# First layer of a delta-rule and attention stack: the gate product as one rounded product over 96 rows, and the second half of the output projection in two parts

## The chip, the cores and the metric

One core of one Trainium2 chip runs the whole program. The time is the device time of one execution, in microseconds (us); lower is better. Engines are named as in the profile: PE (TensorE matmuls), PEld (its weight loads), DVE (VectorE), ACT (ScalarE), POOL (GpSimd), SP (SyncE, which issues transfers here).

## The reference

The program computes four layers on x of 16 batches x 512 tokens x 512 features; the change touches only the first one. Of that one:

```python
q = silu(x @ Wq.T); k = silu(x @ Wk.T); v = x @ Wv.T      # 16 heads of 32
beta = 2.0 * sigmoid(x @ Wbeta.T)
k = k * rsqrt(sum(k * k, -1) + EPS)
o = delta_rule(q, k, v, beta)                # a state per head, carried over the 512 tokens
gate = sigmoid(x @ Wg1.T @ Wg2.T)            # Wg1 is 32 x 512, Wg2 is 512 x 32
og = o * gate; og = og * rsqrt(mean(og * og, -1) + EPS) * g_norm
x = x + og @ Wo.T                            # x was layer-normalised on the way in
```

The gate is a product of two thin matrices: g1 = x @ Wg1.T has 32 features, and the gate product takes them to 512.

## The kernel before, in words

`delta_rule_layer` (from line 47) works on spans of 256 tokens, two to a batch, 32 in all. Everything is held with features on the partitions. `over_spans` unrolls one step per span, and each step works on up to five spans at once: it finishes `now` (solve, chain over chunks of 64 tokens), writes out `behind`, inverts triangles for `ahead`, projects `further`, and loads `beyond`. 29 of the 32 steps have both `behind` and `further`, 30 have `further`. Two spans are projected in `begin` before the first step. Nothing loops at run time: every instruction of every step stands in the instruction stream, and the order on each engine is the order of the Python calls. The engines meet through semaphores alone.

Accurate products are made of rounded ones: a number is split into its rounded part (`_hi`, type fp32r) and the rest (`_lo`), and `split3` (lines 38 to 42) adds hi x hi, hi x lo and lo x hi. All large projections go that way (features, `project_k`, `project_q`, `project_gb`, `project_v`, `output`). A few small ones are plain fp32 products instead, `project_gate` (L542) among them; the profile records each plain fp32 product as two matmuls and two weight loads. The products of the solve, of `query_corrections` (L646), `transitions` (L658), `without_state` (L682), `state_inputs` (L692) and `chain` (L703 and L709) are also plain fp32, and tiny: 32 to 64 rows, 32 to 64 columns, 64 products a call (16 and 16 in a chain call).

PE's order in a step from the end of the solve on: `project_gb(further)`, `query_corrections(now)` (L646), `output(behind, 0)` (12 products of 512 columns), `transitions(now)` (L658), `project_q(further, 1)` (24 of 256), `without_state(now)` (L682), `output(behind, 1)` (12 of 512), `state_inputs(now)` (L692), `chain(now, 0)`, `key_sums(further, 0)` (L529), `chain 1`, `project_gate(further, 0)`, `chain 2`, `project_gate(further, 1)`, `chain 3`, `key_sums(further, 1)`, `output_sums(now)` (L719), then `project_v`, `key_rows` (L557), `triangles` (L569) and `project_v`. A chain call adds gt x state for the next state (L703), then the state's part of the output (L709); call c + 1 waits for `state_ready`, which DVE gives in `advance` (L933), before the gated output (L939).

PSUM banks are shared by hand. BB holds g1 and beta of `project_gb`, then `output(behind, 1)`, then half of the gate; so `output(behind, 1)` waits until ACT has taken beta, and `project_gate(further, 1)` until DVE has added the residual (`add_residual`, L953).

ACT's `take_gb` copies g1 (L313) and makes beta (L316) out of BB. DVE fills its free time with the columns of the inverse of `ahead` (`invert`, L886 and L889), cut into named stretches that stand between the steps that PE waits for. SP loads and stores and carries triangles and inverses through DRAM.

## Time and profile before

| | |
|---|---|
| median of 3 runs | 4955.77 us (4949.72 to 4962.0) |
| profiled execution, its own time | 4960.62 us |
| its span, first to last instruction | 4958.5 us |
| PE busy | 4588.3 us, 93% |
| DVE busy | 3635.6 us, 73% |
| ACT busy | 2411.9 us, 49% |
| first layer | about 0 to 2010 us of the span |
| granted clock, mean | 0.969 |

Busy time counts from the start of an instruction to its end. PE's are pipelined and overlap, so the distance from the start of one to the start of the next says what it costs in a row of them. "issue" as the end of idle time means that the engine waited for nothing that the profile shows.

### The profile page before, as it was taken

The page shows a single profiled execution, that of the slowest core. Times are in us where ns is not written, and L with a number is a line of the kernel's source. Part 1 is how long each engine was busy: PE and PEld are TensorE (multiplying, and loading weights), DVE is VectorE, ACT ScalarE, POOL GpSimd, SP SyncE. Part 2 cuts the span into 40 slices and gives each one's busy share as a digit, 9 for nine tenths or more (in the row PEclk, how much of TensorE's full clock was granted, in tenths as well). Part 3 has the DMA queues.
Part 4 walks back from the last instruction along what each step waited for, and adds up shares of the span by engine and source line. Part 5 has one row for each costly group of instructions (what it writes and reads, how often), then busy time and mean ns, then how long its engine had stood idle before and what let it go on. Part 6 is the DMA issues. An engine that isn't in the chain of part 4 may idle for free.

```text
span 4958.5 us, 144788 instructions
## 1 busy us (share of the span) xinstructions
PE 4588.3 (93%) x63104; PEld 3209.3 (65%) x63104; DVE 3635.6 (73%) x7890; ACT 2411.9 (49%) x4592; POOL 720.6 (15%) x909
## 2 busy tenths in 40 slices
PE   7999999999999998699999999999999999999998
PEld 7787777777787776555655654664664665565564
DVE  6677777766676665578778778778778877877876
ACT  3333343333343332366466456457456546546645
POOL 0000000000000000121221221221221122122121
PEclk8999999999999998899999999999999999999999
DMA  2222222222222221100000000000000000000000
GB/s 85 55 63 72 64 69 65 67 67 66 65 63 63 63 63 49 62 2 18 18 1 19 18 2 18 18 2 18 18 18 2 18 18 2 18 18 2 18 10 10
DMA packets 352134, 171.76 MB, mean 35 GB/s; under 512 B 300016, under 2 KB 300784, under 8 KB 350736
## 3 DMA queue, kind: packets, MB, share of 16 engines
q1 hardware_dynamic: 342528, 145.20, 10.9%
q10 hardware_dynamic: 8976, 17.30, 1.2%
q8 instruction: 499, 8.18, 0.7%
q14 instruction: 131, 1.07, 0.1%
HBM read 93.74 MB, written 67.63 MB: 33 GB/s over the span
## 4 chain that ended last, share of the span: by engine, by line
PE 43%; DVE 11%; ACT 2%; issue 1%; POOL 1%; DMA 1%; SPq 0%; DVEq 0%; ACTq 0%; POOLq 0%
PE row_psum L1738 9%; PE row_psum L1713 9%; PE row_psum L40 5%; DVE smax L2000 5%; PE row_psum L42 5%; PE row_psum L41 5%; PE row_psum L1726 4%; PE row_psum L1786 1%; DVE xr_lo L1861 1%; PE row_psum L1766 1%; DVE probs L1980 1%; PE row_psum L1500 1%; DVE stats L1827 1%; POOL rstd L1297 1%; DMA q_stack<-shift 1%
## 5 line engine op out<-in xcount | busy, mean ns | idle before, releaser
L2000 DVE TENSOR_REDUCE smax<-row_psum 128x1 f32<-128x512 f32 x2048 | 1270.5, 685 | 91.7 <-PE row_psum L1713 88.6
L1434 ACT ACTIVATE probs<-row_psum 128x512 f32<-128x512 f32 x2048 | 1091.8, 603 | 352.2 <-PE row_psum L1726 332.9
L1713 PE MATMUL row_psum<-k_stack,q_stack 64*128 64x512 f32 (+1 forms) x2048 | 738.1, 437 | 50.8 <-DVE smax L2000 24.5
L1726 PE MATMUL row_psum<-q_stack,k_stack 64*128 64x512 f32 (+1 forms) x2048 | 733.3, 458 | 22.6 <-ACT probs L1434 8.1
L1713 PEld LDWEIGHTS row_psum<-k_stack,q_stack 64*128 64x128 f32 (+1 forms) x2048 | 350.8, 186 | 503.8 <-DVE smax L2000 372.9
L1738 PE MATMUL row_psum<-probs,v_aug 128*32 128x512 f32 x4096 | 538.9, 603 | 1.6 <-ACT av_sb L1450 0.4
L1726 PEld LDWEIGHTS row_psum<-q_stack,k_stack 64*128 64x128 f32 (+1 forms) x2048 | 319.3, 184 | 225.8 <-ACT probs L1434 155.7
L889 DVE TENSOR_TENSOR lane_t<-lane_t,lane_p 128x30 f32<-128x30 f32 (+14 forms) x960 | 318.5, 332 | 32.9
L40 PE MATMUL row_psum<-wf_hi,xr_hi 128*128 128x320 f32 (+1 forms) x1024 | 331.9, 324 | 4.7 <-DVE xr_lo L1861 3.2
L886 DVE TENSOR_TENSOR lane_p<-lane_t 128x30 f32<-128x30 f32 (+14 forms) x960 | 316.4, 330 | 23.5
L42 PE MATMUL row_psum<-wf_hi,xr_lo 128*128 128x320 f32 (+1 forms) x1024 | 319.0, 312 | 0.0
L41 PE MATMUL row_psum<-wf_lo,xr_hi 128*128 128x320 f32 (+1 forms) x1024 | 317.9, 310 | 0.0
L265 POOL TENSOR_TENSOR o_lo<-og_both,o_hi 128x512 fp32r<-128x512 f32 x64 | 93.2, 1476 | 1331.3 <-DVE tri L904 1239.1
L1311 POOL TENSOR_TENSOR xs<-xs,av_n 128x256 f32<-128x256 f32 x128 | 94.0, 735 | 1236.1 <-DVE av_n L1994 1236.1
L369 ACT ACTIVATE og_both<-og_both 128x512 f32<-128x512 f32 x64 | 40.4, 632 | 470.6 <-DVE og_both L939 470.6
L1401 ACT ACTIVATE q_stack<-row_psum 128x512 fp32r<-128x512 f32 x256 | 153.8, 607 | 152.7 <-PE row_psum L1663 151.2
L40 PE MATMUL span_bank<-x_hi,w_hi 128*128 128x256 f32 x768 | 223.9, 292 | 0.0
L41 PE MATMUL span_bank<-x_lo,w_hi 128*128 128x256 f32 x768 | 214.4, 279 | 1.1 <-issue 1.1
L42 PE MATMUL span_bank<-x_hi,w_lo 128*128 128x256 f32 x768 | 214.4, 279 | 1.1 <-issue 1.1
L1990 DVE RECIPROCAL av_rc<-row_psum 128x16 f32<-128x16 f32 x128 | 32.2, 251 | 245.6 <-PE row_psum L1786 245.6
L40 PEld LDWEIGHTS row_psum<-wf_hi,xr_hi 128*128 128x128 f32 x1024 | 192.9, 188 | 29.1 <-issue 20.6
L41 PEld LDWEIGHTS row_psum<-wf_lo,xr_hi 128*128 128x128 f32 x1024 | 193.7, 189 | 0.6
(215 smaller groups left out, 9999.8 us busy)
## 6 DMA issues: line engine op xcount, KB each, us to landing
x_sp<-in_x ACTq DMA_DIRECT2D x33, 512.0 KB, 4.2
tri_dram<-tri SPq DMA_DIRECT2D x256, 64.0 KB, 2.0
lane_t<-tri_dram SPq DMA_DIRECT2D x32, 512.0 KB, 4.6
inv_dram<-lane_t SPq DMA_DIRECT2D x32, 512.0 KB, 2.7
inv_b<-inv_dram SPq DMA_DIRECT2D x256, 64.0 KB, 2.3
x_res<-in_x SPq DMA_DIRECT2D x32, 512.0 KB, 3.8
x<-x_res SPq DMA_DIRECT2D x32, 512.0 KB, 3.9
xs<-x SPq DMA_DIRECT2D x16, 1024.0 KB, 5.5
```

Source lines behind the costliest of these rows:

```text
L40: pe.matmul(out, a_hi, b_hi, start=first, stop=False)
L41: pe.matmul(out, a_hi, b_lo, start=False, stop=False)
L42: return pe.matmul(out, a_lo, b_hi, start=False, stop=last)
L886: mark(dve.tensor_tensor(prod, lane_t[:, 0:m, m:m + 1].to_broadcast([P, m, n]), lane_t[:, m:m + 1, m + 1:NB].to_broadcast([P, m, n]), ALU. ...
L889: mark(dve.tensor_tensor(lane_t[:, 0:m, m + 1:NB], lane_t[:, 0:m, m + 1:NB], prod, ALU.add))
L1311: pool.tensor_tensor(xq, xq, av_n[:, :, :, :].rearrange("p t h e -> p t (h e)"), ALU.add).then_inc(adot_added, 1)
L1401: act.activation(q_stack[:, m, :], ps[:, (HP + m) % STACK_BANKS, :], ACT.Copy).then_inc(qstack_ready, 1)
L1434: act.activation(probs[:, h % PROBS, tt, :], ps[:, m % STACK_BANKS, :], ACT.Exp, scale=float(DH) ** -0.5).then_inc(exp_ready, 1)
L1713: pe.matmul(ps[:, bank, :], q_stack[rows, qt, P * st:P * st + P], k_stack[rows, kv, :], start=True, stop=True).then_inc(max_mm, 1)
L1726: pe.matmul(ps[:, m % STACK_BANKS, :], k_stack[rows, kv, P * tt:P * tt + P], q_stack[rows, qt, :], start=True, stop=True).then_inc(score_m ...
L1738: last = pe.matmul(ps[32 * e:32 * e + 32, 6, :], v_aug[:, tt, h % NKV, :], probs[:, h % PROBS, tt, :], start=tt == 0, stop=tt == NT - 1)
L2000: dve.tensor_reduce(smax[:, g, st:st + 1], ps[:, bank_of("max", NT * g + st), :], AX.X, ALU.max).then_inc(max_ready, 1)
```

## The change

Three edits, all in the first layer. The gate product takes one rounded product with 96 rows in place of a plain fp32 product with 32: rows 0 to 31 hold g1 rounded, 32 to 63 the rest of g1, 64 to 95 g1 rounded once more, against weights rounded, rounded and rest. ACT makes the third part by a copy, DVE the second by a subtraction; the weights are loaded three times and split once at the start. The second half of the output projection runs two of its four input blocks before `state_inputs` and two after. DVE adds the residual of that half after `advance(now, 0)`.

```diff
-        g2 = sb("g2", [HD, D])
+        g2 = sb("g2", [3 * HD, D], F32R)
-        g1_beta = sb("g1_beta", [HD + H, SPAN])
-        g1, beta_t = g1_beta[0:HD, :], g1_beta[HD:HD + H, :]
+        g1 = sb("g1", [3 * HD, SPAN], F32R)
+        beta_t = sb("beta_t", [H, SPAN])
...
-            sp.dma_start(g2[:, :], w_g2).then_inc(c_in, 16)
+            for part in range(3):
+                sp.dma_start(g2_raw[HD * part:HD * part + HD, :], w_g2).then_inc(c_in, 16)
...
+            def split_g2():
+                act.wait_ge(c_in, 128)
+                act.activation(g2[:, :], g2_raw, ACT.Copy).then_inc(w_hi_ready, 1)
...
             def take_gb(b, s, first=False):
                 act.wait_ge(gb_proj, at(b, s, 1, 1))
-                act.activation(g1, BB[0:HD, 0:SPAN], ACT.Copy).then_inc(g1_ready, 1)
+                act.activation(g1[0:HD, :], BB[0:HD, 0:SPAN], ACT.Copy).then_inc(g1_ready, 1)
                 if not first:
                     act.wait_ge(beta_out, at(b, s, 16, 0))
-                act.activation(beta_t, BB[HD:HD + H, 0:SPAN], ACT.Tanh, scale=0.5).then_inc(beta_ready, 1)
+                act.activation(beta_t[:, :], BB[HD:HD + H, 0:SPAN], ACT.Tanh, scale=0.5).then_inc(beta_ready, 1)
+                act.wait_ge(g1_ready, at(b, s, 2, 1))
+                act.activation(g1[2 * HD:3 * HD, :], g1[0:HD, :].bitcast(F32), ACT.Copy).then_inc(g1_ready, 1)
...
             def project_gate(b, s, n, behind=None):
                 if n == 0:
                     pe.wait_ge(q_ready, at(b, s, 2, 1))
-                    pe.wait_ge(g1_ready, at(b, s, 1, 1))
+                    pe.wait_ge(g1_ready, at(b, s, 2, 2))
+                    pe.wait_ge(g1_lo_ready, at(b, s, 1, 1))
...
                     last = pe.matmul((BA, BB)[n][:, SPAN * g:SPAN * g + SPAN], g2[:, P * f:P * f + P],
-                                     g1, start=True, stop=True)
+                                     g1[:, :], start=True, stop=True)
...
-            def output(b, s, t, further, ahead):
+            def output(b, s, t, further, ahead, inputs=range(KT)):
-                if further:
+                if further and inputs[0] == 0:
                     if t == 0:
                         pe.wait_ge(ksilu_ready, at(*further, 2, 2))
                     else:
                         pe.wait_ge(beta_ready, at(*further, 1, 1))
+                        pe.wait_ge(g1_lo_ready, at(*further, 1, 1))
...
-                pe.wait_ge(ohi_ready, at(b, s, TS, t + 1))
-                pe.wait_ge(olo_ready, at(b, s, TS, t + 1))
-                for k in range(KT):
+                if inputs[0] == 0:
+                    pe.wait_ge(ohi_ready, at(b, s, TS, t + 1))
+                    pe.wait_ge(olo_ready, at(b, s, TS, t + 1))
+                for k in inputs:
...
-                last.then_inc(wo_mm, 1)
+                if inputs[-1] == KT - 1:
+                    last.then_inc(wo_mm, 1)
...
             begin (PE), each span:
-                    pe.wait_ge(c_in, 96)
+                    pe.wait_ge(c_in, 128)
+                    pe.wait_ge(w_lo_ready, 4)
...
                 without_state(*now)
                 if behind:
-                    output(*behind, 1, further, ahead)
+                    output(*behind, 1, further, ahead, range(KT // 2))
                 state_inputs(*now)
+                if behind:
+                    output(*behind, 1, further, ahead, range(KT // 2, KT))
                 chain(*now, 0)
...
+            def split_g2(place):
+                rows = slice(2 * HD, 3 * HD)
+                dve.wait_ge(w_hi_ready, place)
+                dve.tensor_tensor(g2[rows, :], g2_raw[rows, :], g2[rows, :].bitcast(F32), ALU.subtract).then_inc(w_lo_ready, 1)
...
+            def split_g1(b, s):
+                dve.wait_ge(g1_ready, at(b, s, 2, 1))
+                dve.tensor_tensor(g1[HD:2 * HD, :], BB[0:HD, 0:SPAN], g1[0:HD, :].bitcast(F32), ALU.subtract).then_inc(g1_lo_ready, 1)
...
                 correct_queries(*now)
+                if further:
+                    split_g1(*further)
                 invert_ahead("queries")
                 if behind:
                     add_residual(*behind, 0)
                 invert_ahead("transitions")
+                invert_ahead("inputs")
+                advance(*now, 0)
                 if behind:
                     add_residual(*behind, 1)
-                invert_ahead("inputs")
-                advance(*now, 0)
                 invert_ahead("chain0")
```

## Rows read from the trace of the kernel before

**Rows 1.** The page: span, busy times, and the queue that carries PE's instructions.

```profile
span 4958.5 us, 144788 instructions
PE 4588.3 (93%) x63104; PEld 3209.3 (65%) x63104; DVE 3635.6 (73%) x7890; ACT 2411.9 (49%) x4592; POOL 720.6 (15%) x909
...
q8 instruction: 499, 8.18, 0.7%
```

**Rows 2.** Windows, middle of the first layer: busy (x count) of PE, PEld, DVE, ACT, POOL.

```profile
190.00:1900.00 1710.00, 1629.09 (x41658) 1347.19 (x41656) 1199.49 (x2951) 655.73 (x1138) 107.53 (x112) 0.96 0.26 65
```

**Rows 3.** ACT's copy of g1, one a step: least, median, most ns, first and last start.

```profile
L313 ACT ACTIVATE g_beta<-span_bank x28: 376/376/377, 239.3 to 1863.0; 32x256 f32<-32x256 f32 x28
```

**Rows 4.** Groups of PE, 200 to 1900 us, with the idle time before them.

```profile
L709 PE MATMUL span_bank<-q_eff,state 32*32 32x64 f32 x3616 | 88.7, 235 | 20.8 <-issue 20.7
L703 PE MATMUL span_bank<-state,gt 32*32 32x32 f32 x3616 | 58.9, 202 | 16.7 <-issue 16.7
```

**Rows 5.** Timeline of PE, dense stretch of one step: start, length, line, count [idle].

```profile
1010.63 1.48 PE L646 MATMUL span_bank<-tri,uw 64*32 64x64 f32 x128
...
1024.91 0.45 PE L703 MATMUL span_bank<-state,gt 32*32 32x32 f32 x32
1025.18 0.30 PE L709 MATMUL span_bank<-q_eff,state 32*32 32x64 f32 x4
1027.06 0.64 PE L709 MATMUL span_bank<-q_eff,state 32*32 32x64 f32 x28 [1.58 <-issue]
1027.62 1.13 PE L529 MATMUL span_bank<-sq,head_ones 128*128 128x512 f32 x2
1028.68 0.45 PE L703 MATMUL span_bank<-state,gt 32*32 32x32 f32 x32
```

**Rows 6.** DMA over 1023.5 to 1032.7 us, 40 slices; then the queue over 190 to 1900.

```profile
GB/s 0 0 0 0 71 0 0 0 249 383 392 410 410 374 45 18 0 0 0 0 71 0 71 178 125 107 276 321 401 374 276 98 27 27 0 0 0 0 71 0
...
q8 instruction: 327, 5.36, 1.3%
```

**Rows 7.** Windows from the end of one such stall to the end of another.

```profile
970.85:1027.05 56.20, 53.47 (x1400) 45.13 (x1401) 41.07 (x100) 23.02 (x40) 3.85 (x4) 1.00 0.28 69
1027.05:1065.11 38.06, 34.27 (x761) 27.54 (x761) 22.00 (x50) 18.73 (x31) 2.94 (x2) 1.00 0.37 86
```

**Rows 8.** Timeline of PE at the second gate call of the same step.

```profile
1031.62 1.12 PE L542 MATMUL span_bank<-g_beta,g 32*128 32x256 f32 x4
1032.68 0.23 PE L703 MATMUL span_bank<-state,gt 32*32 32x32 f32 x3
```

**Rows 9.** Timeline of PE, end of a rounded projection of 256 columns.

```profile
1001.95 0.28 PE L41 MATMUL span_bank<-x_lo,w_hi 128*128 128x256 f32 x1
1002.07 0.28 PE L42 MATMUL span_bank<-x_hi,w_lo 128*128 128x256 f32 x1
1002.27 0.24 PE L587 MATMUL span_bank<-uw,tri 32*32 32x64 f32 x1
```

**Rows 10.** Timeline of DVE, same step.

```profile
1012.15 1.42 DVE L923 TENSOR_TENSOR q_eff<-kq,span_bank 128x256 f32<-128x256 f32 x4 [0.54 <-PE span_bank L646]
1023.79 0.69 DVE L953 TENSOR_TENSOR x_res<-x_res,span_bank 128x512 f32<-128x512 f32 x1 [0.40 <-PE span_bank L42]
1026.48 0.28 DVE L933 TENSOR_TENSOR state<-state,span_bank 128x128 f32<-128x128 f32 x1
1029.65 0.42 DVE L939 SCALAR_TENSOR_TENSOR og_both<-gate,span_bank 128x256 f32<-128x256 f32 x1
1036.25 0.20 DVE L895 COPY lane_t<-lane_b 128x32 f32<-128x32 f32 x1
```

**Rows 11.** Timeline of ACT, same step, after beta.

```profile
1013.60 0.60 ACT L320 ACTIVATE kq<-span_bank 128x512 f32<-128x512 f32 x1 [2.08 <-DVE q_eff L923]
```

**Rows 12.** Timeline at the start: PE's first gate, DVE's last weight split.

```profile
30.55 1.99 PE L542 MATMUL span_bank<-g_beta,g 32*128 32x256 f32 x8
...
26.05 2.29 DVE L822 TENSOR_TENSOR w_lo<-tri,w_hi 128x2048 fp32r<-128x2048 f32 x1 [0.66 <-ACT w_hi L288]
```

More of the change, by code:

```diff
@@ L106, in delta_rule_layer @@
         lane_t = sb("lane_t", [P, NB, NB])
+        g2_raw = lane_t[0:3 * HD, :, :].rearrange("p j i -> p (j i)")[:, D:2 * D]
         stage_gb = lane_t[:, :, :].rearrange("p j i -> p (j i)")[:, 0:KT * (HD + H)]
@@ L128, in delta_rule_layer @@
         xlo_ready = sem("xlo_ready"); kproj = sem("kproj"); ksilu_ready = sem("ksilu_ready")
-        gb_proj = sem("gb_proj"); g1_ready = sem("g1_ready")
+        gb_proj = sem("gb_proj"); g1_ready = sem("g1_ready"); g1_lo_ready = sem("g1_lo_ready")
         beta_ready = sem("beta_ready"); beta_out = sem("beta_out"); res_loaded = sem("res_loaded")
@@ L193, in to_lanes @@
                 sp.dma_start(beta_dram.rearrange("u h i -> h u i"),
-                             beta_t.rearrange("h (u i) -> h u i", i=NB)).then_inc(beta_out, 16)
+                             beta_t[:, :].rearrange("h (u i) -> h u i", i=NB)).then_inc(beta_out, 16)
                 for t in range(TS):
@@ L402, in begin @@
                     if span is first:
-                        split_weight(WV, c_in, 96)
+                        split_g2()
+                        split_weight(WV, c_in, 128)
                     take_k(*span, 1)
                     if span is first:
-                        split_weight(WO, c_in, 96)
+                        split_weight(WO, c_in, 128)
                     take_gb(*span, first=span is first)
@@ L755, in begin @@
                     key_sums(*span, 1)
-                    pe.wait_ge(w_lo_ready, NW + 1)
+                    pe.wait_ge(w_lo_ready, NW + 2)
                     project_v(*span, 0)
@@ L961, in begin @@
                 split_gb(3)
-                split_weight(WV, 4)
-                split_weight(WO, 5)
-                dve.wait_ge(c_in, 96)
+                split_g2(4)
+                split_weight(WV, 5)
+                split_weight(WO, 6)
+                dve.wait_ge(c_in, 128)
                 mark(dve.tensor_scalar(gnorm_half[:, :], gnorm_half[:, :], 0.5, None, ALU.mult))
+                split_g1(*first)
                 statistics(*second)
@@ L970, in begin @@
                 split_x(*second)
+                split_g1(*second)
                 statistics(*third)
```

## The prediction

> **What bounds the kernel now.** I read the page first: PE is busy 93% of the span [rows 1]. The windows view then shows the first layer by itself: between 190 and 1900 us PE is busy 1629.1 of 1710 us [rows 2], DVE 1199.5 and ACT 655.7. PE bounds this layer, and every step waits for PE's order. A step takes (1863.0 - 239.3) / 27 = 60.14 us [rows 3], and 29 steps are affected by all of the change.
>
> The second thing to see is what PE's idle time is. The groups view puts 20.8 and 16.7 us of it before L709 and L703, nearly all ended by "issue" [rows 4]. The timeline shows one case: in the middle of a row of equal products, after 4 of 32 records of L709, PE stands still for 1.58 us, and no semaphore is waited for there in the code [rows 5]. I take this for a lack of instructions. Three facts carry it. The queue named "instruction" moves 8.18 MB in 499 packets, 16 KB each [rows 1], and PE has 126,208 recorded instructions, so one packet is close to 253, say 256 with the unrecorded waits. Between the ends of such stalls the records of PE and PEld are 2801 and 1522 [rows 7]; with some 15 semaphore instructions each (the code's waits put about 16 into a step) these are 11 and 6 times 256. And the DMA slices of 0.23 us show single packets (71 GB/s in a slice) near 1024.5, 1028.2 and 1032.3 us [rows 6]: the stall of 1027.06 ends some 2.5 us after a packet started, and the next packet starts 1.1 us after the stall's end. So a block of 256 instructions is asked for when PE's queue enters the block before it, and can be used about 3.7 us later (3.6 to 4.1 between packets). A block that PE runs through in less ends in a stall.
>
> Where can that be? A step has 1468 matmul records, as many loads and 16 waits: 2952 instructions, 11.5 blocks [327 packets for 28.4 steps, rows 6]. From `query_corrections` at 1010.63 [rows 5] to the end of the chain, 0.93 us behind 1032.68 [rows 8], stand 826 records, or 6.5 blocks, in 23.0 us: with the stall of 1.58 taken off, 21.4 us of work, 3.3 us a block. That is below 3.7. The two groups of rows 4 alone have (20.8 + 16.7) / 28.4 = 1.3 us of idle a step; from start to start, which also counts what a record's drawn-out end covers, and over all groups, I put the stalls at 2.3 us a step and the step without them at 58.0.
>
> **The gate product.** Before: from its first record to the next chain's is 1.06 us for 4 records [rows 8], twice a step, 2.11 us in all. After: 2 records each. A rounded product of 256 columns costs 0.12 us in a row, and 0.20 where tiny products follow [rows 9]. With 0.12 + 0.20 for each pair and some 0.03 for the first's start: 0.35 us twice a step, hence 2.11 - 0.70 = 1.4 at the least. But the old 1.06 holds a start and a hand-over too, and without them the new pair is 0.24; so at most 2.11 - 0.24 = 1.87. I take 1.75, nearer to the upper end, for records of the old product lie 0.22 apart inside it, and the rest of its time is start and hand-over that stay hidden in neither. 30 steps and two spans of `begin`. In `begin` the 8 records take 1.99 us [rows 12]; I take 1.4 us off each.
>
> **Its price.** ACT gets one copy of 32 x 256: 0.38 us [rows 3] and a wait for its own earlier copy. ACT then idles 2.08 us until q_eff [rows 11], so it costs nothing; without that cover it would be 0.38 x 30 = 11 us. DVE gets a subtraction of 32 x 256 out of PSUM: at least 0.28 (L933, 128 columns), at most 0.42 (L939, 256 columns) [rows 10]; I take 0.4, the same column count. It is placed right behind q_eff (1012.15 to 1013.57) and delays the inverse and the residual behind it in DVE's queue. DVE has 0.40 us idle before the residual of the second half [rows 10], which the move frees as well, so it fits; without cover 12 us. PE's new wait before `output(behind, 1)` asks for this subtraction, done by about 1014 (q_eff ends at 1013.6), while that product starts some 3 us before its end at 1023.8 [rows 10]; so nothing stands queued behind a real wait. At the start, two more transfers on SP and two small splits come before DVE's last split ends at 28.3 us; g1's rest is then ready near 29.3, the gate starts at 30.55 [rows 12]. Nothing.
>
> **The move.** Six products (1.5 us) go from before `state_inputs` to behind it. PE's work is the same. For DVE the state of chunk 0 is taken at 1026.48, though PE had its part of it done by 1025.4: the residual (0.69) and its wait (0.40) stood before it [rows 5, 10]. With the residual behind `advance`, DVE is ready. That gives PE nothing where `key_sums` (1.06 us) lies between chain 0 and chain 1 anyway; it pays for the subtraction. On SP the store of `behind` goes 3 us later, behind it the load of 512 KB (the two busy stretches of slices in rows 6) and `from_lanes`, which waits for the inverse until 1036.4 [rows 10] in any case; nobody waits longer. The other effect is on blocks: `state_inputs` and chain 0 are the densest run (192 records in 2.4 us), and 1.5 us of slow products between them lets one block arrive. Lower bound 0, upper bound the stalls in that run, about 1 us a step; since the block count and the work of the whole stretch stay, I take 0.2.
>
> **What the blocks give back.** The stretch loses 1.75 us and four records: 19.6 us for 6.45 blocks, 3.0 us each. Were it bound by blocks alone it would take 6.45 x 3.7 = 23.9 us, no less than now, and the gain would be nought; were there no such bound, all of 1.75 would arrive. Between the ends I walked a step, block by block: the time from 40 instructions ahead of a block's edge to the next edge, against 3.7 us (4.2 in the solve, where transfers are dense; 40 is my choice, since with it the walk meets the measured step). For before this gives 60.4 us a step against 60.1 measured. After, a step has 2952 - 8 + 1 = 2945 instructions (one more for the fourth wait of `output`), which is 11 blocks and 129: the edges fall in two sets of places in turn, half a block apart, and hardly drift. One set has an edge at the end of `without_state` and one before the second gate: 885 to 1012 in records has 2.9 us of work (0.8 us stall), 1140 to 1267 has 2.6 (1.1 us). The other set falls better. The walk gives about 60.5 and 58.5 us in turn, 59.5 on average, so 0.9 us less a step, 2.3 us of stalls having become 3.2.
>
> The Trainium skill (Runtime: NRT & Kernel Launch, "Instruction fetch mechanics") gives the same 16 KiB blocks, but says that the fetch is hidden because the sequencer issues more slowly than blocks arrive. The rows speak against it here. By that rule the gate's whole saving would arrive: rival 1.
>
> **Sum**, against the profiled execution: 29 x 0.93 = 27, the first step (gate alone) 1, `begin` 2.8, DVE now binding by about 0.1 us between chains 2 and 3 (its 0.28 + 0.42 [rows 10] and 0.6 of inverse are 1.3 us a link against PE's 1.2) gives back 3. Together -28: 4960.6 becomes 4932.6. That execution lay 4.85 us above the median, so 4928 as a median. The last steps and the other layers stay.
>
> **Rivals.**
> 1. The saving arrives whole: 30 x 1.75 + 2.8 = 55, to 4901. For it: the stalls fall in other engines' shadow; the move spreads blocks. Against it: the counts in multiples of 256 [rows 7]. With all present chain stalls gone too it would be 4875; I give that little.
> 2. The blocks take all: the stretch stays as long as it is, only `begin` gains, and DVE's 3 us come on top: 4955.8 - 2.8 + 3, or up to 5 us less: about 4953. For it: packets come every 3.6 to 4.1 us without a pause in the dense stretch.
> 3. Slower: DVE becomes the bound between q_eff and chain 0. It has under 1.5 us idle there [rows 10], and the subtraction with its wait costs 0.4 to 0.9. If the blocks take all and DVE is late by 0.8 us before chain 1, 30 x 0.8 = 24 - 3: 4977. It decides from the point where the state of chunk 0 is given later than `key_sums` ends. Against it: the residual leaves the same place.
> 4. It does not do what it says: a product over 96 rows at the old cost. 4955. The rounded products of 128 rows in the same stream speak against it.
>
> **Chances.** Forecast (4913 to 4941) 0.55; rival 1 0.23; rival 2 0.14 with rival 4; rival 3 0.05; the rest lies between. A measurement of this kernel tells about 0.3%, 15 us, from no change. Faster by more: 0.81, same 0.14, slower 0.05. The range reaches from near rival 1 to near rival 2: 4897 to 4948.
>
> **What would show it.** L542 with 128 records, chain to chain 0.3 us over a gate. Stalls ended by "issue" grow in the chain to 3 us a step, ends of stalls still multiples of 256 apart, long and short steps in turn. DVE waits for L703 less. Wrong if steps are all 58.4 us (rival 1), or if "issue" takes 4 us a step (rival 2), or if PE waits for DVE's state by 0.5 us or more (rival 3).

## The result, and the profile after the change

The median of four runs is 4903.71 us (4896.4 to 4908.7), beside 4952.75 us for four runs of the kernel before. The ratio is 0.9897 with a 95% interval of 0.9876 to 0.9917. That is 51 us faster by the ratio, where 28 were forecast: the direction was right and the time lies in the range, but the size was forecast at about half.

The profiled execution took 4907.11 us. The page of the kernel after answers to [rows 1]:

```profile
span 4905.3 us, 144631 instructions
PE 4526.2 (92%) x62976; PEld 3166.9 (65%) x62976; DVE 3651.2 (74%) x7923; ACT 2423.4 (49%) x4625; POOL 720.1 (15%) x909
q8 instruction: 499, 8.18, 0.7%
```

PE has 128 products and 128 loads fewer (four a step and in each span of `begin`), DVE and ACT 33 instructions more. The instruction queue still moves 499 packets. The first layer is where all of it happened: the next layer's first product starts at 1969.5 us, before it was 2022.8. From there to the end both kernels take the same time (2935.8 and 2935.7 us).

Next the windows of the middle of that layer, as [rows 2], ACT's copy of g1 once a step, as [rows 3], and PE's groups from 200 to 1900 us, as [rows 4]:

```profile
190.00:1900.00 1710.00, 1608.94 (x42735) 1336.39 (x42734) 1248.64 (x3069) 679.59 (x1187) 111.37 (x115) 0.98 0.26 67
...
L319 ACT ACTIVATE g<-span_bank x28: 375/375/375, 236.7 to 1817.0; 32x256 fp32r<-32x256 f32 x28
...
L719 PE MATMUL span_bank<-q_eff,state 32*32 32x64 f32 x3744 | 80.3, 217 | 5.5 <-issue 5.5
L713 PE MATMUL span_bank<-state,gt 32*32 32x32 f32 x3713 | 60.7, 195 | 31.0 <-issue 29.4 <-DVE state L958 1.7
L702 PE MATMUL span_bank<-uw,rhs 64*32 64x32 f32 x3712 | 41.8, 200 | 14.3 <-issue 13.8
L552 PE MATMUL span_bank<-g 96*128 96x256 f32 x112 | 28.1, 332 | 0.0
```

A step takes (1817.0 - 236.7) / 27 = 58.53 us, 1.6 less than before. Three things are to be seen. L552 has no idle time of its own: the gate product is cheap. The idle time ended by "issue" has not gone: it moved from L709 (now L719, 20.8 to 5.5) to the chain's other product (16.7 to 31.0) and to L702, `state_inputs` (1.5 to 14.3). And two numbers changed that the prediction gave no term: one L719 product takes 217 ns where it took 235 in [rows 4], and the granted clock, the column behind POOL, rose to 0.98 from 0.96 [rows 2].

PE in one step of the kernel after, at the two gate calls:

```profile
1016.63 0.50 PE L552 MATMUL span_bank<-g 96*128 96x256 f32 x2
1017.06 0.45 PE L713 MATMUL span_bank<-state,gt 32*32 32x32 f32 x32
1017.34 0.66 PE L719 MATMUL span_bank<-q_eff,state 32*32 32x64 f32 x32
1017.93 0.50 PE L552 MATMUL span_bank<-g 96*128 96x256 f32 x2
1018.36 0.39 PE L713 MATMUL span_bank<-state,gt 32*32 32x32 f32 x24
1019.82 0.23 PE L713 MATMUL span_bank<-state,gt 32*32 32x32 f32 x5 [1.07 <-issue]
```

A gate call, start to start, is 0.43 us, both times (1.06 in [rows 8]). The stall at 1019.82 is one of those that the prediction reads as a missing block of 256 instructions. The windows from stall to stall bear this out in the new kernel:

```profile
1011.98:1019.82 7.84, 6.77 (x255) 4.78 (x255) 5.14 (x17) 0.63 (x1) 0.00 (x0) 1.00 0.19 70
1019.82:1128.57 108.75, 103.92 (x2674) 87.38 (x2673) 80.43 (x194) 46.20 (x81) 7.71 (x8) 0.98 0.27 67
```

255 + 255 records and two or three semaphore instructions are two blocks, in 7.84 us: 3.9 us each, inside the 3.6 to 4.1 of the prediction. 2674 + 2673 records and some 30 semaphore instructions (17 are recorded in a step, and this is 1.86 steps) are 21 blocks.

The whole trace says it more sharply. Number every instruction of PE in its recorded order (loads, products, semaphore instructions), and take for each place of the step the usual gap to the next product. In 28 steps 53 gaps are over 0.6 us longer than usual in the kernel after, and all 53 stand at the same remainder of the division by 256 (192 or 193). In the kernel before it is 43 of 45, at the same remainder.

DVE took the subtraction and the new order as forecast. In the same step it reaches the state of chunk 0 with 1.20 us to spare, and the residual follows it:

```profile
1014.44 0.29 DVE L958 TENSOR_TENSOR state<-state,span_bank 128x128 f32<-128x128 f32 x1 [1.20 <-PE span_bank L713]
1014.89 0.42 DVE L964 SCALAR_TENSOR_TENSOR og_both<-gate,span_bank 128x256 f32<-128x256 f32 x1 [0.17 <-PE span_bank L719]
1015.23 0.68 DVE L978 TENSOR_TENSOR x_res<-x_res,span_bank 128x512 f32<-128x512 f32 x1
```

### The profile page after: what moved, and what is told of

It is laid out like the page before. It is cut to its first block, busy times and chain, and to the rows that moved or that the text cites. A ratio compares the mean times of both kernels' runs of the same rounds, so it can differ in the third digit from the quotient of the medians.

```text
span 4905.3 us, 144631 instructions
## 1 busy us (share of the span) xinstructions
PE 4526.2 (92%) x62976; PEld 3166.9 (65%) x62976; DVE 3651.2 (74%) x7923; ACT 2423.4 (49%) x4625; POOL 720.1 (15%) x909
## 4 chain that ended last, share of the span: by engine, by line
PE 44%; DVE 11%; ACT 2%; issue 1%; POOL 1%; DMA 1%; SPq 0%; DVEq 0%; ACTq 0%; POOLq 0%
PE row_psum L1743 10%; PE row_psum L1768 9%; PE row_psum L40 5%; PE row_psum L42 5%; PE row_psum L41 5%; DVE smax L2030 5%; PE row_psum L1756 4%; PE row_psum L1816 1%; DVE xr_lo L1891 1%; PE row_psum L1796 1%; DVE probs L2010 1%; PE row_psum L1530 1%; DVE stats L1857 1%; POOL rstd L1327 1%; PE row_psum L1715 1%
## 5 line engine op out<-in xcount | busy, mean ns | idle before, releaser
L1391 ACT ACTIVATE probs<-row_psum 128x64 f32<-128x64 f32 x256 | 52.0, 228 | 291.7 <-PE row_psum L42 291.7
```

## What half a clock looks like in the kernel before

To see where the missing 23 us came from I went back to the trace of before. PE in one step, timeline:

```profile
1269.09 0.38 PE L703 MATMUL span_bank<-state,gt 32*32 32x32 f32 x20
1271.06 0.28 PE L703 MATMUL span_bank<-state,gt 32*32 32x32 f32 x11 [1.60 <-issue]
...
1274.57 2.07 PE L542 MATMUL span_bank<-g_beta,g 32*128 32x256 f32 x4
1276.57 0.65 PE L703 MATMUL span_bank<-state,gt 32*32 32x32 f32 x32
```

and windows over the same time:

```profile
1262.00:1269.00 7.00, 7.00 (x282) 5.95 (x280) 6.11 (x17) 0.60 (x1) 0.00 (x0) 1.00 0.02 5
1269.00:1271.00 2.00, 0.46 (x38) 0.31 (x25) 1.61 (x5) 0.00 (x0) 0.00 (x0) 1.00 0.68 257
1271.00:1273.00 2.00, 1.94 (x46) 0.90 (x45) 1.21 (x4) 0.00 (x0) 0.00 (x0) 0.86 0.15 26
1273.00:1276.00 3.00, 3.00 (x68) 2.42 (x68) 1.16 (x4) 0.63 (x1) 0.00 (x0) 0.50 0.58 169
```

PE stands still for 1.6 us on a missing block, ending at 1271.06. Up to there the granted clock was 1.00 (2.4 GHz). It falls within the next 2 us and then stays at 0.50 (1.2 GHz), and the gate call takes 2.00 us in place of 1.06. Of the 56 gate calls between 200 and 1900 us in the kernel before, 14 took over 1.3 us (most of these about 2.0), so the mean is 1.28 us where the median is 1.06. In the kernel after all 56 calls take 0.43 or 0.44.

Over 28 steps, from the second `query_corrections` on, the clock records show 137 us at half clock before and 61 after. Of these, 106 before and 10 after lie in the chain, what stands between its links and `output_sums`; the rest (31 and 51) lies in `triangles` and mostly in the products right behind it, and grew. If work at half clock takes at most twice its time, as the gate calls do, at most half of such a stretch is lost: (137 - 61) / 2 = 38 us is the most that the clock can have given back here.

What was lost can also be summed from the trace: for each product at half clock, its distance to the next one beyond the usual distance (the median) at that place of the step at full clock, block edges left out. That is 2.0 us a step before and 0.9 after, 30 us in 28 steps. This is the term that the prediction doesn't have.

The clock also differs from execution to execution of one kernel, and the time goes with it. Of 23 executions of the kernel before on one chip, the fastest had a mean granted clock of 0.972, the slowest 0.965:

```
4938.84 us, clock 0.972      4975.59 us, clock 0.965
correlation of time and clock over the 23: -0.88; straight line: 3.4 us for 0.001 of clock
the same over 17 and 13 executions on two other chips: 2.4 and 3.7 us for 0.001
```

I use 3.4 us for 0.001 below as a second estimate of what the clock is worth. It is a correlation. No run here sets the clock and leaves all else.

## The experiments

Each ratio is to the kernel before, run on the same chip between the runs of the variant. The steps come from the copy of g1 (28 starts, 27 steps) of the profiled execution. "Stalls" are my sum, from start to start, over the block edges of 28 steps. "Clock" is the mean of the mean granted clocks of all executions, and beside it stands the mean ns of one product of the chain with q_eff, which a clock fall in the chain draws out. "Lost" is what half clock costs in a step, summed as above. Step, stalls, lost and ns come from the profiled execution alone. It lay 12 us above the median of its kernel in e1, 12 below in e3 and 10 above in e10, and e4, with the work of after but for two terms, lost 0.4 us less: so much a single execution leaves open.

| kernel | ratio (95%) | step us | stalls us | lost us | clock | ns |
|---|---|---|---|---|---|---|
| before | 1 | 60.14 | 2.3 | 2.0 | 0.967 to 0.968 | 235 |
| e1 gate alone | 0.9950 (0.9932 to 0.9967) | 59.64 | 3.2 | 1.5 | 0.971 | 230 |
| e2 move alone | 0.9926 (0.9905 to 0.9946) | 58.79 | 2.0 | 0.5 | 0.976 | 221 |
| e3 move, PE's side alone | 0.9992 (0.9979 to 1.0006) | 60.10 | 2.0 | 0.8 | 0.973 | 223 |
| e5 move, DVE's side alone | 0.9967 (0.9954 to 0.9980) | 59.77 | 2.3 | 1.4 | 0.971 | 228 |
| after | 0.9897 (0.9876 to 0.9917) | 58.53 | 2.7 | 0.9 | 0.977 | 217 |
| e4 after, gate over 32 rows | 0.9888 (0.9865 to 0.9910) | 58.26 | 2.8 | 0.5 | 0.975 | 217 |
| e6 all twelve products behind | 0.9991 (0.9980 to 1.0002) | 59.75 | 3.3 | 1.6 | 0.971 | 216 |
| e7 three parts | 0.9942 (0.9928 to 0.9956) | 59.50 | 3.1 | 0.8 | 0.977 | 217 |
| e8 after, padded | 0.9869 (0.9853 to 0.9884) | 57.79 | 2.0 | 0.8 | 0.976 | 217 |
| e9 after, padded twice | 0.9918 (0.9895 to 0.9941) | 59.06 | 2.8 | 1.0 | 0.976 | 220 |
| e10 before, padded | 1.0002 (0.9986 to 1.0018) | 60.76 | 2.5 | 2.3 | 0.969 | 241 |
| e11 three parts, padded | 0.9880 (0.9852 to 0.9907) | 58.16 | 2.1 | 0.8 | 0.976 | 220 |

### e1: the gate product alone

```diff
 (the kernel after, with the output and the residual back in their old places)
                 if behind:
-                    output(*behind, 1, further, ahead, range(KT // 2))
+                    output(*behind, 1, further, ahead)
                 state_inputs(*now)
-                if behind:
-                    output(*behind, 1, further, ahead, range(KT // 2, KT))
```

> The gate product of the change alone; output(behind, 1) in one piece and the residual where it stood before. Theory A (the gate brings nearly all: shorter product, and no half-clock stretches in the chain any more): 38 to 45 us less than before, about 4911, steps of 58.8 us, less than 20 us at half clock between chain 0 and the end of the chain. Theory B (the move does away with the half clock, by cutting the long stalls): 25 to 32 us less, about 4924, long stalls in chain 0 and about 100 us at half clock in the chain as before. The prediction's walk by blocks says 19 us less.

Measured: 4935.88 us, 25 us faster (0.9950). So the gate product doesn't bring the whole gain. The groups of PE, 200 to 1900 us, show what it pays:

```profile
L719 PE MATMUL span_bank<-q_eff,state 32*32 32x64 f32 x3616 | 84.7, 230 | 18.9 <-issue 18.9
L713 PE MATMUL span_bank<-state,gt 32*32 32x32 f32 x3616 | 62.0, 200 | 42.2 <-issue 42.2
```

In the chain's first group the idle time ended by "issue" goes from 16.7 [rows 4] to 42.2 us: 25.5 us over 28 steps, or 0.9 a step (the other group gives 1.9 us back). That is the size of what the walk gave (2.3 to 3.2 us a step). The stretch became shorter and ran into its blocks. The gain has the size of theory B, but 51 us at half clock are left in the chain, half of before, which neither theory had.

### e2: the move alone

```diff
 (the kernel before)
-                    output(*behind, 1, further, ahead)
+                    output(*behind, 1, further, ahead, range(KT // 2))
                 state_inputs(*now)
+                if behind:
+                    output(*behind, 1, further, ahead, range(KT // 2, KT))
...
-                if behind:
-                    add_residual(*behind, 1)
                 invert_ahead("inputs")
                 advance(*now, 0)
+                if behind:
+                    add_residual(*behind, 1)
```

> The move alone (PE's split of output(behind, 1) and DVE's new place for the residual), gate as before. Theory A: 3 to 8 us less than before, about 4947, half-clock stretches in the chain still there. Theory B: 18 to 25 us less, about 4931, half-clock stretches in the chain mostly gone. Both: stalls that lay in chain 0 (0.9 us a step) go down by half and come up in state_inputs.

Measured: 4924.39 us, 37 us faster (0.9926). The move is worth more than the gate product by itself, and more than any theory gave it. The prediction had 0.2 us a step, 6 us. Windows, copy of g1 and groups of this kernel:

```profile
190.00:1900.00 1710.00, 1633.91 (x42839) 1349.38 (x42839) 1228.51 (x3030) 662.13 (x1151) 110.47 (x114) 0.99 0.27 66
...
L709 PE MATMUL span_bank<-q_eff,state 32*32 32x64 f32 x3713 | 83.9, 221 | 7.3 <-issue 7.3
L703 PE MATMUL span_bank<-state,gt 32*32 32x32 f32 x3744 | 57.8, 196 | 6.8 <-issue 6.7
L692 PE MATMUL span_bank<-uw,rhs 64*32 64x32 f32 x3712 | 41.9, 200 | 11.9 <-issue 11.3
```

Of the 1.35 us a step, the stalls give 0.3. They went from the two chain groups (37.5 us before, 14.1 now) in part to `state_inputs` (1.5 to 11.9). The rest is the same work done faster: the clock over the stretch is 0.99 against 0.96 [rows 2], and the time at half clock over 28 steps fell from 137 to 34 us (in the chain from 106 to 23). What it cost fell by 1.5 us a step, 42 us in all. Over all executions the clock rose by 0.0095, at 3.4 us for 0.001 an estimate of 32 of the 37 us. Both ways the clock is most of the gain. They don't divide it more finely: 1.5 and 0.3 us a step are 0.4 more than the step gained.

### e3 and e5: the two sides of the move

e3 has the new order on PE and the residual where it was; e5 has the old order on PE and the residual behind `advance` of chunk 0.

```diff
 (e3, the kernel before)
-                    output(*behind, 1, further, ahead)
+                    output(*behind, 1, further, ahead, range(KT // 2))
                 state_inputs(*now)
+                if behind:
+                    output(*behind, 1, further, ahead, range(KT // 2, KT))
 (e5, the kernel before)
-                if behind:
-                    add_residual(*behind, 1)
                 invert_ahead("inputs")
                 advance(*now, 0)
+                if behind:
+                    add_residual(*behind, 1)
```

> PE's split alone, DVE's residual still ahead of the state of chunk 0. The product then ends 1.2 us later, DVE waits for it, adds the residual (0.69) and two columns of the inverse... six instructions (2 us) before the state, so PE should wait for the state in front of chain 1 by 0.5 to 1 us a step: 15 to 30 us slower than the move with both halves, about 4965 to 4975. If DVE has more slack than I read, it equals the move with both halves within 5 us.

> Before, with DVE's residual of the second half behind the state of chunk 0 and nothing else changed (output(behind, 1) in one piece ahead of state_inputs). If the move's gain came from PE's long stall in chain 0 being cut and the half-clock stretches going with it, this changes little: same as before within 8 us, about 100 us at half clock in the chain as before. If it came from DVE giving the state of chunk 0 earlier, it gives most of the 36 us of the move: about 4925.

Measured: e3 4958.42 us, no difference from before (0.9992), and 34 us above e2 (15 to 30 were expected). e5 4940.67 us, 16 us faster (0.9967), between the two cases of its expectation. The waits of PE and of DVE in e3 say why:

```profile
PE span_bank L703 <- DVE state L937: 19.8, 27, 1.1
PEld span_bank L703 <- DVE state L937: 42.9, 28, 2.0
DVE x_res L957 <- PE span_bank L42: 78.7, 28, 4.9
```

PE now gives the output late, DVE waits for it (4.9 us at most, in every step) with the state of chunk 0 queued behind, and PE waits for the state in 27 of 28 steps, by 19.8 us on its products and 42.9 on its loads. The clock gain of the split is there (235 to 223 ns, 1.2 us a step less lost at half clock), and the wait eats it. So one side of the move needs the other: PE's order alone is worth nothing, and DVE's alone 0.33%. With DVE's side in place PE's adds 0.41% more.

e5 also refutes a sentence of the prediction, that DVE's readiness "gives PE nothing". In the kernel before PE's loads did wait for the state of chunk 0 at times:

```profile
PEld span_bank L703 <- DVE state L933: 8.3, 11, 0.8
```

e5 has no such wait, and after has 2.1 us in two. These are waits of loads, which run ahead of the products, so they need not be time of the same length; the products of before don't wait for this state. What the half clock cost fell by 0.5 us a step in e5, 15 us in 28 steps, which is about all of its gain. Why an earlier state keeps the clock up, no run shows.

### e4: do 96 rows cost more than 32?

This kernel takes the gate product over the 32 rows of rounded part by rounded part, and leaves out the two correction terms.

```diff
-                    last = pe.matmul((BA, BB)[n][:, SPAN * g:SPAN * g + SPAN], g2[:, P * f:P * f + P],
-                                     g1[:, :], start=True, stop=True)
+                    last = pe.matmul((BA, BB)[n][:, SPAN * g:SPAN * g + SPAN], g2[0:HD, P * f:P * f + P],
+                                     g1[0:HD, :], start=True, stop=True)
```

> The changed kernel with the gate product over the first 32 rows only: the two correction terms are left out, all copies and waits stay. If a rounded product costs by its columns alone, the same time as the changed kernel, about 4904 within 5 us. If 96 rows cost more than 32, up to 0.2 us a product, 60 of them pairs: 10 to 25 us less.

Measured: 4905.72 us, 0.9888 (0.9865 to 0.9910), beside 0.9897 for after: the same. The correction terms in the same product are free on PE. Rival 4, a product over 96 rows at the old cost, is set aside by the gate call's 0.43 us.

### e6 and e7: other places for the second half

e6 puts all of the second half behind `state_inputs`. e7 keeps six products before it, and puts three behind it and three behind chain 1, with the residual behind `advance` of chunk 1.

```diff
 (e6, the kernel after)
-                if behind:
-                    output(*behind, 1, further, ahead, range(KT // 2))
                 state_inputs(*now)
                 if behind:
-                    output(*behind, 1, further, ahead, range(KT // 2, KT))
+                    output(*behind, 1, further, ahead)
 (e7, the kernel after)
-                    output(*behind, 1, further, ahead, range(KT // 2, KT))
+                    output(*behind, 1, further, ahead, range(2, 3))
...
                 chain(*now, 1)
+                if behind:
+                    output(*behind, 1, further, ahead, range(3, 4))
```

> The changed kernel with all 12 products of output(behind, 1) behind state_inputs. without_state and state_inputs are then 256 records in 2.7 us, two blocks: the stall moves there, 1.3 us or more a step in state_inputs against 0.7, and chain 0 has none. Blocks alone: 5 to 15 us slower than the changed kernel. If the half clock comes from the stall alone wherever it lies, it comes back (over 50 us at half clock); if it comes from tiny products with a stall among them behind no long products, it stays away, since 2.8 us of long products follow.

> The changed kernel with output(behind, 1) in three parts: two input blocks ahead of state_inputs, one behind it, one between chain 1 and the first gate product, the residual behind the state of chunk 1. If blocks of 256 instructions set the pace of the chain, 0.75 us of three long products among it cuts the stalls of chain 2 and 3 (1.0 us a step) by half or more: 10 to 20 us faster than the changed kernel, about 4890. If DVE binds instead, the residual ahead of the state of chunk 2 makes PE wait before chain 3 and it is 5 to 15 us slower.

Measured: e6 4949.31 us (0.9991), some 47 us above after by the ratios, where 5 to 15 were expected. e7 4927.78 us (0.9942), some 22 us above after, where a gain was expected. Both were misses. The timeline and the group of e6:

```profile
911.32 1.12 PE L702 MATMUL span_bank<-uw,rhs 64*32 64x32 f32 x105
914.94 0.31 PE L702 MATMUL span_bank<-uw,rhs 64*32 64x32 f32 x18 [2.50 <-issue]
...
L702 PE MATMUL span_bank<-uw,rhs 64*32 64x32 f32 x3584 | 43.0, 202 | 57.5 <-issue 57.5
```

Without the six slow products between them, `without_state` and `state_inputs` stand back to back: 256 tiny products with 256 loads, two whole blocks in 2.6 us of work. A stall of up to 2.5 us stands in the second, 57.5 us in 28 steps. So the first six products are needed where they are as much as the last six. The stalls are not all of it: they cost 0.6 us a step more than in after, and half clock 0.6 to 0.7 more. The expectation had put the question whether half clock comes back when the stall lies ahead of long products. It does: 102 us in 28 steps against 61 in after, 47 of them in the twelve products of `output` that follow, and nearly none in the chain.

e7's chain is as good as after's (L719 at 217 ns), but its block edges fall in `solve_third`. Its waits of PE:

```profile
PE span_bank L597 <- DVE og_both L941: 17.3, 12, 3.0
PE span_bank L719 <- issue: 13.6, 13, 1.5
PE span_bank L702 <- issue: 12.5, 20, 1.2
PE span_bank L605 <- issue: 12.1, 7, 2.1
```

In after L597 waits for DVE once (0.4 us) and L605 for 0.6 us. `solve_third` takes 0.8 us more a step, and the steps alternate: 61.8, 58.0, 61.7, 57.5, 60.5, 57.8. That is the pattern that two sets of edges half a block apart give, as the prediction had it for after, where it is faint (58.7 and 58.4 on average). The wait put down to DVE may in part be a missing block that ended later than DVE did; the trace doesn't divide them. That the edges' place is the matter, and not the third part, is what e11 tests.

### e8 to e11: the same work, its block edges elsewhere

If blocks of 256 instructions cause the stalls, then instructions added once, at the start of PE's program, move every edge in every later step, and cost next to nothing themselves.

```diff
             def begin(first, second, third):
+                for _ in range(64):
+                    pe.wait_ge(first_in, 32)
```

These waits are met long before the second one is reached. 64 of them add 32 instructions to PE's 127,740 by the records, so two go into one. e9 has 128 waits, 64 instructions. e10 is the kernel before and e11 is e7, each with the 64 waits of e8.

> The changed kernel with 64 more waits on a semaphore that is long complete, once, in PE's stream at the very start: 32 or 64 instructions of a few us in all, and nothing else differs afterwards. If stalls lie at the edges of blocks of 256 instructions, every stall of every later step lies 32 or 64 instructions earlier in the step's order than in the changed kernel, ends of stalls stay multiples of 256 apart counted from the start of the stream, and the mean step moves by up to 0.5 us either way (15 us). If the stalls belong to places in the code, they stay where they are and the time stays within 3 us.

> The changed kernel with 128 such waits at the start, 64 instructions by the count of the 64 waits that gave 32. A step is 11.5 blocks long (2945 instructions), so the edges stand in two sets of places, and this shifts both by 64. A walk through the step with the stage lengths of the changed kernel's trace gives, against the changed kernel, 0.3 us a step less for 32 instructions (measured: 0.7 less) and 0.7 more for 64: 15 to 20 us slower than the changed kernel, 30 us slower than with 32, about 4922, with stalls of 3 us a step or more. If the gain of the first padding had another cause (a later start of PE), this one is as fast or faster: 4892 or less.

> The kernel before with the same 32 instructions at the start. Its step is 2952 instructions, 11 blocks and 136, so the edges wander over 16 pairs of places within the 29 steps whatever the start: same as before within 5 us, stalls 2.3 us a step. If padding helps by itself, it is 10 to 20 us faster.

> Three parts of output(behind, 1), with the same 32 instructions at the start. The version without them has steps of 61.7 and 57.3 us in turn, its stalls in chain 0 and in the third part of the solve in every second step. If those are a matter of where the edges fall, the slow steps get shorter and it comes to the padded changed kernel or below: 4885 to 4895. If the later residual and store are what costs it (its transfers then meet the packets of the solve), it stays 10 us or more above it: 4905 or more.

Measured: e8 4891.79 us, the fastest of all (0.9869). e9 4916.85 us (0.9918). e10 4959.45 us (1.0002). e11 4897.99 us (0.9880), 0.62% below e7, but not below e8. First e8, its copy of g1 and four of its waits of PE, then a wait of e9:

```profile
L319 ACT ACTIVATE g<-span_bank x28: 375/375/375, 238.5 to 1798.8; 32x256 fp32r<-32x256 f32 x28
...
PE span_bank L713 <- issue: 25.8, 37, 1.5
PE span_bank L702 <- issue: 11.5, 26, 0.8
PE span_bank L597 <- DVE og_both L941: 5.3, 2, 4.8
PE span_bank L719 <- issue: 2.4, 2, 1.6
```

```profile
PE span_bank L719 <- issue: 30.3, 38, 1.8
```

e8's step is 57.79 us, 0.74 less than after's, and its stalls 2.0 us against 2.7. Over 27 steps that is 20 us; behind them one wait of 4.8 us for DVE gives some back in this execution, and the medians differ by 12 us. The intervals of e8 and after just overlap (0.9876 to 0.9884), so that e8 is faster than after isn't shown by the times alone; the steps' difference has the same sign. The stalls moved as expected: in e8 43 of 44 gaps of over 0.6 us beyond the usual stand at the same remainder of 256 as in after, which is 32 instructions earlier in the step. e9's edges fall in the q_eff products (30.3 us against after's 5.5 and e8's 2.4), and it is clearly slower than e8 (30 us were expected, 24 came by the ratios), though not clearly slower than after. So the same instructions in the same order, moved against the block grid by 32 or 64, differ by 0.5%. The block reading explains that; a reading by the work alone can't. For the kernel before the shift by 32 changed nothing, as was expected: its step of 2952 instructions moves the edges by 136 each time, so over 29 steps they visit places 8 apart all through the block, from any start. A step of 2945 moves them by 129, so they stay in two narrow bands, and there the start matters. e11 came out 3 us above what was expected of it and well below the 4905 of its rival.

## Why the prediction was right or wrong

**Right: the bound and the blocks.** PE bounds the layer, the rest of the program stays to within 0.1 us, and the stalls are missing blocks of 256: [rows 7], the gaps at one remainder of 256 in before, after and e8, and the shifts of e8 and e9 all say so. The Trainium skill (Runtime: NRT & Kernel Launch, "Instruction fetch mechanics") holds that the fetch is hidden behind the sequencer's issue rate. The measured 7.84 us for two blocks and the 57.5 us of e6 say that here it isn't. The stalls grew, as forecast: from 2.3 to 2.7 us a step after, and to 3.2 in e1, where 3.2 was forecast for after.

**Right: the cover.** ACT's copy and DVE's subtraction (0.41 us in `begin`, 0.4 forecast) cost nothing that is seen, the rows of the product are free (e4), and rival 3, PE waiting for DVE's state by 0.5 us or more, appears as a rule of every step only in e3, where half of the move is missing: 19.8 us on products and 42.9 on loads in 28 steps. In after it happens twice, by 1.2 us at most.

**Wrong: "since the block count and the work of the whole stretch stay, I take 0.2" for the move.** Those 6 us measured 37 alone, and 26 on top of the gate product (0.9897 / 0.9950 = 0.9947). Nor did the 0.2 enter the sum: the walk takes only the gate's 1.75 off the stretch, and its 0.9 is the sum's 0.93. The bound named there, "the stalls in that run, about 1 us a step", was a bound on stalls alone. What failed is the sentence before the number: the work's time does not stay when the work does. Behind about half of the long stalls in the chain TensorE's clock stood at half for some time, and what ran then ran slower. With fewer such stretches the chain's products and the gate calls got shorter in e2, though their records are the same (235 to 221 ns; 1.28 to 1.11 us on average). [rows 2] held the hint, a clock of 0.96, and other steps of the same trace had it too, with gate calls of 2.00 us against the 1.06 of the one step that was read.

**Wrong, in the other direction: the gate product at 1.75 us a step.** At full clock it is 2 x (1.056 - 0.431) = 1.25, below the lower end of 1.4. A pair in this stream takes 0.43, where rows of other places had suggested 0.32 to 0.35. All gate calls together did get shorter by 1.7 us a step (2 x (1.28 - 0.43)), which looks like the forecast, but 0.45 of that is the half clock in a quarter of the old calls: the number by luck, not the reason. And **the walk's 3.2 us of stalls** was 0.5 too high for after. Both places that it named have their stalls, 0.7 us a step in `state_inputs`, behind `without_state`, and 0.7 beside the second gate; it was too high in the rest.

Over 28 steps from start to start, in us a step (the measured parts: gate calls at full clock, block edges, what half clock cost, and what is left):

```
                          forecast     measured
gate product               -1.75        -1.25
stalls                     +0.9         +0.4
half clock                  0           -1.1
what is left               -0.1         +0.3
together                   -0.93        -1.64    (parts rounded)
```

Two errors of half a microsecond cancelled by luck, so the gate and the blocks together came out as forecast (0.85 us less in both columns). The third line is the one that moved the time. The missing part is 0.71 x 29 = 21 us. The half clock holds 30 us by the sum over products, and some 24 by the estimate of 3.4 us for 0.001 (0.976 against 0.969 in the two profiled executions).

**Rival 1** gave a step of 58.4, and the step is 58.5. Yet the mechanism is not its: the stalls did not become cheaper, they grew, and the gate saving did not arrive whole (e1). A step length alone would have confirmed the wrong cause.

## What stays open

How much of the 37 us of e2 is the clock and how much PE's waits is worked out in two ways, from the products' distances in one execution and from a correlation over executions, not from a run with the clock alone changed. Nor is it settled what makes the clock fall. I counted PE's standstills of over 1.7 us, start to start, in the chain and `state_inputs`: 11 before, 6 of them followed by half clock; 17 (12) in e1; 29 (14) in e6; 2 (1) in e2; 5 (2) in after; none in e8. Of short ones, 0.9 to 1.3 us, at most one of some 99 was followed by it in kernels with the new gate product, but 18 of 64 in kernels with the old one. So in these counts half clock goes with long standstills, and with short ones only where the old gate product stands. No run parts these two, and none explains the half clock behind `triangles`.

## What to carry to other kernels

Where PE runs hundreds of tiny products, price an edit in three currencies: its own time at full clock, where the blocks of 256 instructions then fall, and how much of it runs at half clock behind PE's standstills; the last was worth some 24 to 30 us here, beside 35 of the first (1.25 x 28). Try slow products between dense runs, on both sides of each (e6 shows what taking one away costs), and move the partner engine's work with them (e3 against e2). Before a variant is judged, try it with its program shifted by some instructions: the grid alone was worth 0.5% between e8 and e9, as much as the gate product by itself.

## What I had not expected of the hardware

- A shift of PE's whole program by 32 instructions that do nothing came out 0.2 to 0.3% faster than none and one by 64 a little slower than none (both within the intervals), and the two differ from each other by 0.5%. The shift by 32 has the lowest time of all: 4891.79 us, 0.9869 (0.9853 to 0.9884).
- Executions of one program on one chip differ by 37 us, and the granted clock goes with it (0.965 against 0.972).
- A gate call in plain float32 (two products of 256 columns, recorded as four) takes 1.06 us from start to start at full clock and 2.00 at half clock; in the rounded form, the call takes 0.43 us, whether the product is one term in 32 rows or three in 96 (e4).
